# Expert weights split once beside attention, 27 units of 256 rows, and rows added into the output by accumulating scatters

## The reference, cut to what matters

```python
x = layernorm(h).reshape(-1, 512)                       # 2560 rows
top_vals, top_idx = top_k(x @ gate_w.T + gate_b, 2)
routing = softmax(top_vals)
for e in range(8):
    t = x @ w1[e].T + b1[e]                             # 1024 wide
    y = t[:, 0::2] * sigmoid(1.702 * t[:, 0::2]) * (t[:, 1::2] + 1.0)
    ye = y @ w2[e].T + b2[e]
    out += ye * sum(routing * (top_idx == e))           # zero where the row did not choose e
h = h + out
```

## Time and profile before

| | us |
|---|---|
| median of 3 runs (1957.12 to 1961.39) | 1958.84 |
| the profiled execution's own time | 1960.39 |
| its span, first to last instruction | 1958.2 |
| `build_rows`, `project` | about 420 |
| attention | 640 |
| router | 280 |
| experts | 553 |
| combine | 64 |

### The profile page before, as it was taken

How to read it: one execution, slowest core, us unless ns; L and a number is a source line. 1 busy time by engine, 2 the same in 40 slices (tenths; PEclk the granted TensorE clock), 3 DMA queues, 4 the chain that set the end, 5 groups by cost and what they waited for, 6 DMA issues and landing times. The chain is left out here.

```text
span 1958.2 us, 29274 instructions
## 1 busy us (share of the span) xinstructions
PE 1469.5 (75%) x9597; PEld 737.7 (38%) x9597; DVE 1431.0 (73%) x2171; ACT 849.2 (43%) x1520; POOL 528.8 (27%) x264
## 2 busy tenths in 40 slices
PE   0364238729999999999995146974999999999960
PEld 0343113303444444444441012452555555555530
DVE  7976989959888888888881977645666666666645
ACT  4473103313777777777775000012444444444410
POOL 4000116650000000000000122101566666665526
PEclk9876568868999999999998555555999999999985
DMA  4002005652222222222224210105665555565528
GB/s 136 1 1 78 0 0 176 231 171 75 91 89 84 93 85 90 91 86 89 87 92 138 75 31 27 54 27 172 204 203 194 193 192 188 195 197 191 180 77 276
DMA packets 143798, 228.19 MB, mean 117 GB/s; under 512 B 14478, under 2 KB 69646, under 8 KB 143706
## 3 DMA queue, kind: packets, MB, share of 16 engines
q1 hardware_dynamic: 134034, 199.31, 30.5%
q0 software_dynamic: 8752, 28.06, 5.1%
q10 hardware_dynamic: 960, 0.17, 0.0%
HBM read 163.14 MB, written 64.03 MB: 116 GB/s over the span
## 5 line engine op out<-in xcount | busy, mean ns | idle before, releaser
L1254 ACT ACTIVATE pT<-p 128x512 f32<-128x512 f32 x800 | 422.9, 609 | 153.9 <-PE p L1155 151.8
L1227 DVE TENSOR_REDUCE mxa<-p 128x1 f32<-128x512 f32 x640 | 409.8, 682 | 96.1 <-PE p L1137 96.1
L1720 POOL TENSOR_TENSOR wl<-shared,wh 128x2048 bf16<-128x2048 f32 x60 | 255.7, 4290 | 128.5 <-ACT wh L1796 128.5
L1137 PE MATMUL p<-ks,qs 128*128 128x512 bf16 x640 | 250.1, 393 | 39.8 <-DMA vs<-d_v 36.4
L1155 PE MATMUL p<-qs,ks 128*128 128x512 bf16 x640 | 243.3, 380 | 14.2 <-ACT pT L1254 12.9
L1753 PE MATMUL p<-xh,wh 128*128 128x384 bf16 x672 | 220.0, 327 | 1.2 <-DVE xl L1833 1.2
L1753 PE MATMUL p<-xl,wh 128*128 128x384 bf16 x672 | 219.9, 327 | 0.0
L1753 PE MATMUL p<-xh,wl 128*128 128x384 bf16 x672 | 219.9, 327 | 0.0
L682 POOL TENSOR_TENSOR xT<-xT,qcbb_ctx 128x2560 f32<-128x2560 f32 x4 | 17.9, 4475 | 705.9 <-DVE qcbb_ctx L700 705.9
L1173 PE MATMUL p<-pT,vs 128*32 128x128 f32 (+1 forms) x2560 | 205.5, 439 | 1.0 <-ACT pT L1254 1.0
L1850 DVE TENSOR_TENSOR yl<-yf,yh 128x384 bf16<-128x384 f32 x84 | 140.8, 1677 | 48.5 <-ACT yh L1811 48.5
(11 more groups left out here) (326 smaller groups left out, 2349.3 us busy)
## 6 DMA issues: line engine op xcount, KB each, us to landing
shared<-in_w1T SPq DMA_DIRECT2D x42, 1024.0 KB
shared<-in_w2T SPq DMA_DIRECT2D x21, 1024.0 KB
d_y<-yo SPq DMA_DIRECT2D x63, 256.0 KB, 4.8
d_v<-xT SPq DMA_DIRECT2D x20, 512.0 KB, 3.9
vs<-d_v SPq DMA_DIRECT2D x32, 320.0 KB
d_o<-osb SPq DMA_DIRECT2D x32, 320.0 KB, 2.2
d_q<-xn SPq DMA_DIRECT2D x16, 480.0 KB, 2.8
d_k<-xn SPq DMA_DIRECT2D x16, 480.0 KB, 2.8
```

The lines of the kernel that those rows point to most:

```text
L1137: mm = pe.matmul(out, qs[u][:, h, q], ks[u][:, h, 0:512], start=True, stop=True)
L1227: dve.tensor_reduce(mxa[u][:, h, qt:qt + 1], bank, AX.X, ALU.max, negate=True).then_inc(s_mfree, 1)
L1254: act.activation(dst, ps[:, second_bank(c, s)], ACT.Exp).then_inc(s_p, 1)
L1720: pool.tensor_tensor(wl[n % 2][:, k], wf[:, k], wh[n % 2][:, k], ALU.subtract).then_inc(s_wl, 1)
```

## The change

Four things are changed together.

1. **Weights.** While attention runs, GpSimd loads each of the 24 parts of 1 MB of the expert weights (8 experts, 3 parts) by a DMA of its own queue, takes hi by a cast and lo by a subtraction, and stores both to `d_w` (another 1 MB). Part n starts once `s_pv` has reached 5n + 1, one part a group. The staging tiles are `xT4`, which attention leaves free. The expert stage then loads hi and lo ready made, 3 MB of bf16 per unit, in a ring of three buffers, two units ahead, by two DMAs with long rows; ScalarE's L1796 and GpSimd's L1720 are gone.
2. **Units** have 256 slots, and there are 27. The router writes the normed rows to `d_x2` as bf16 hi and lo (ScalarE casts, GpSimd subtracts), so a gather brings both, the turns are bf16 (16 a unit), and hi and lo need no splitting behind them: one copy by ScalarE and one by VectorE, 1024 elements each, take them out of PSUM.
3. **Output.** The router stores the residual `hs` to `d_acc`, and puts into each slot its row (`slot_row`) and its probability (`slot_prob`, carried through the token product as three bf16 parts, so that product has five tables instead of two). In the expert stage VectorE multiplies the second layer by the probability and adds the weighted bias, and GpSimd adds the 128 rows to `d_acc` by an indirect DMA that accumulates in memory. Each such scatter waits for the one before it. At the end `d_acc` is copied to `out`, by two DMAs of SP and two of ScalarE; `combine` is gone.
4. `build_rows` allocates its semaphores directly and clears them behind a barrier of its own.

```diff
+        d_w = dram("d_w", (EXP_N, P, 3 * WPART), BF16)
+        d_acc = dram("d_acc", (TOK + P, L))
...
+        w_first = shared[:].bitcast(BF16)
+        s_w = [[ctx.enter_context(nc.semaphore(f"expert_weights{k}_in{c}")) for k in (1, 2)] for c in range(RING)]
...
+        def load_expert(sp, n, w, free=lambda k: None):
+
+            e = sp.value_load(unit_e[0:1, n:n + 1], min_val=0, max_val=EXP_N - 1)
+            for k, at, end in ((0, 0, 2 * WPART), (1, 2 * WPART, 3 * WPART)):
                 free(k)
-                sp.dma_start(wf[:, k], src.rearrange("e (i p) o -> p (e i) o", p=P)).then_inc(s_w, 16)
+                sp.dma_start(w[:, at:end], d_w[bass.ds(e, 1), :, at:end].rearrange("e p w -> p (e w)")
+                             ).then_inc(s_w[n % RING][k], 16)
...
-        combine(nc, a, locals())
...
+            def load(n):
+                e, k = divmod(n, 3)
+                src = a["w1T"][e, k] if k < 2 else a["w2T"][e]
+                pool.dma_start(wf[n % 2].rearrange("p (i o) -> p i o", i=IT), src.rearrange("(i p) o -> p i o", p=P)
+                               ).then_inc(s_wf[n % 2], 16)
+
+            load(0)
+            load(1)
+            for n in range(3 * EXP_N):
+                u, (e, k) = n % 2, divmod(n, 3)
+                hi, lo = wsplit[u][:, 0:IT * L], wsplit[u][:, IT * L:]
+                pool.wait_ge(s_pv, SPLIT_PACE * n + 1)
+                pool.wait_ge(s_wf[u], 16 * (n // 2 + 1))
+                if n >= 2:
+                    pool.wait_ge(s_wst[u], 16 * (n // 2))
+                pool.tensor_copy(hi, wf[u]).then_inc(s_wsp, 1)
+                pool.wait_ge(s_wsp, 2 * n + 1)
+                pool.tensor_tensor(lo, wf[u], hi, ALU.subtract).then_inc(s_wsp, 1)
+                pool.wait_ge(s_wsp, 2 * n + 2)
+                pool.dma_start(d_w[e, :, k * WPART:(k + 1) * WPART], wsplit[u]).then_inc(s_wst[u], 16)
+                if n + 2 < 3 * EXP_N:
+                    load(n + 2)
...
-UNIT = 384
+UNIT = 256
+RING = 3
+WPART = 2 * IT * L
 UNITS = (TOK * TOPK - EXP_N) // UNIT + EXP_N
...
-                sp.wait_ge(s_xn, COMPS * (b + 1))
-                sp.dma_start(d_x2[b * T:(b + 1) * T].rearrange("(c p) l -> p c l", p=P), xn[:, b % 2]).then_inc(s_x2[b % 2], 16)
+                sp.wait_ge(s_xl, COMPS * (b + 1))
+                sp.dma_start(d_x2[b * T:(b + 1) * T].rearrange("(c p) l -> p c l", p=P),
+                             xb[:, b % 2].rearrange("p c s l -> p c (s l)")).then_inc(s_x2[b % 2], 16)
+            sp.dma_start(d_acc[0:TOK].rearrange("(t p) l -> p t l", p=P), hs[:]).then_inc(s_acc, 16)
             sp.wait_ge(s_unit, 1)
-            load_expert(sp, 0)
+            load_expert(sp, 0, w_first)
...
+                if b >= 2:
+                    act.wait_ge(s_x2[b % 2], 16 * (b // 2))
+                for r in range(b * COMPS, (b + 1) * COMPS):
+                    act.wait_ge(s_xn, r + 1)
+                    act.copy(xb[:, b % 2, r % COMPS, 0], xn[:, r % COMPS]).then_inc(s_xh, 1)
...
-                mm = pe.matmul(ps[:, 2, 0:2 * COLS], lane_is[:, n], col_is[:, n].rearrange("p s c -> p (s c)"),
+                mm = pe.matmul(ps[:, 2, 0:NS * COLS], lane_is[:, n], col_is[:, n].rearrange("p s c -> p (s c)"),
...
-                    if b >= 2:
-                        dve.wait_ge(s_x2[b % 2], 16 * (b // 2))
-                        dve.wait_ge(s_turn, COMPS * (b - 1))
                     for r in range(b * COMPS, (b + 1) * COMPS):
-                        dve.tensor_scalar(xn[:, b % 2, r % COMPS], hs[:, r], mv[:, r, 0:1], sd[:, r:r + 1],
+                        if b >= 1:
+                            dve.wait_ge(s_xl, r - COMPS + 1)
+                            dve.wait_ge(s_turn, r - COMPS + 1)
+                        dve.tensor_scalar(xn[:, r % COMPS], hs[:, r], mv[:, r, 0:1], sd[:, r:r + 1],
                                           ALU.subtract, ALU.mult).then_inc(s_xn, 1)
...
+            chain(dve.tensor_copy(pparts[:, 0], prob[:]))
+            chain(dve.tensor_tensor(prest, prob[:], pparts[:, 0], ALU.subtract))
+            chain(dve.tensor_copy(pparts[:, 1], prest))
+            chain(dve.tensor_tensor(pparts[:, 2], prest, pparts[:, 1], ALU.subtract))
...
+            for n in range(3):
+                chain(dve.tensor_tensor(col_is[:, :, 2 + n], col_is[:, :, 1],
+                                        pparts[:, n].unsqueeze(2).broadcast_to([P, PAIRS, COLS]), ALU.mult))
...
+            chain(dve.tensor_scalar(idf, found[:, 1], -float(P), None, ALU.add))
+            chain(dve.scalar_tensor_tensor(idf, found[:, 0], float(P), idf, ALU.mult, ALU.add))
+            chain(dve.tensor_scalar(slot_token[:], idf, 0.0, None, ALU.max))
+            chain(dve.tensor_scalar(no_row[:], my_lane[:], float(TOK + P), None, ALU.add))
+            chain(dve.tensor_scalar(empty, found[:, 0], 0.0, None, ALU.is_equal))
+            chain(dve.scalar_tensor_tensor(slot_row[:], empty, no_row[:], idf, ALU.mult, ALU.add))
+            chain(dve.tensor_copy(slot_prob[:], found[:, 2]))
+            chain(dve.tensor_tensor(slot_prob[:], slot_prob[:], found[:, 3], ALU.add))
+            chain(dve.tensor_tensor(slot_prob[:], slot_prob[:], found[:, 4], ALU.add))
...
+            def load_weights(n):
+                def free(k):
+                    if n >= RING and k == 0:
+                        sp.wait_ge(s_g1, IT * (n - RING + 1))
+                    if n >= RING and k == 1:
+                        sp.wait_ge(s_g2, Q * (n - RING + 1))
+
+                load_expert(sp, n, w_flat[n % RING], free=free)
...
+                    sp.wait_ge(s_yo, Q * (n - RING + 1))
...
+            sp.wait_ge(s_sc, 16 * Q * NU)
+            for h in range(0, 4, 2):
+                rows = slice(h * TOK // 4, (h + 1) * TOK // 4)
+                sp.dma_start(rows_out[rows], d_acc[rows]).then_inc(s_out, 16)
+            sp.wait_ge(s_out, 16 * 4)
...
-                    pool.wait_ge(s_tx, IT * n)
+                c = n % RING
+                if n >= RING:
+                    pool.wait_ge(s_tx, Q * (n - RING + 1))
                 for q in range(Q):
...
+                    pool.indirect_dma_start(xg[c][:, q], None, d_x2, bass.IndirectOffsetOnAxis(slot_token[:, Q * n + q:Q * n + q + 1], 0)
+                                            ).then_inc(s_xg[c], 16)
 
             gather(0)
+            gather(1)
+            pool.wait_ge(s_acc, 16)
             for n in range(NU):
-                if n + 1 < NU:
-                    gather(n + 1)
-                    for k in range(3):
-                        weight_lo(n + 1, k)
+                if n + 2 < NU:
+                    gather(n + 2)
+                for q in range(Q):
+                    j = Q * n + q
+                    pool.wait_ge(s_yo, j + 1)
+                    if j >= 1:
+                        pool.wait_ge(s_sc, 16 * j)
+                    pool.indirect_dma_start(d_acc, bass.IndirectOffsetOnAxis(slot_row[:, j:j + 1], 0), yo[j % OUTS][:], None,
+                                            compute_op=ALU.add).then_inc(s_sc, 16)
...
+            def turn(i, c):
+                pe.wait_ge(s_xg[c % RING], 16 * Q * (i + c // RING + 1))
                 for q in range(Q):
...
+                n = num(i, c)
+                pe.wait_ge(s_xa, n + 1)
+                pe.wait_ge(s_xd, n + 1)
+                pe.wait_ge(s_w[c][0], 16 * (i + 1))
                 for o in range(IT):
-                    wait(pe, s_yf, i, c, IT, o - 1)
+                    if not first:
+                        pe.wait_ge(s_yf, IT * (n - 1) + o + 1)
...
+                        out = ps[:, 2 + o, k * UNIT:(k + 1) * UNIT]
...
+                                mm = pe.matmul(out, w[c][:, k, ws, t, cols], x[c][:, t, xs], start=t == 0 and m == 0,
                                                stop=t == IT - 1 and m == 2)
                     mm.then_inc(s_g1, 1)
-                pe.wait_ge(s_wl, count(i, c, 3, 3))
+                if not last:
+                    turn(i, c + 1)
+                pe.wait_ge(s_w[c][1], 16 * (i + 1))
...
+                            pe.wait_ge(s_yl, IT * n + t + 1)
+                        for m, (ws, ys) in enumerate(PRODUCTS):
+                            mm = pe.matmul(ps[:, 6 + q], y[c][:, t, ys, q * P:(q + 1) * P], w[c][:, 2, ws, t],
...
+                for q in range(Q):
+                    if not first:
+                        pe.wait_ge(s_yo, Q * (n - 1) + q + 1)
                     second(q, range(IT - 1))
-                for q in range(2):
+                for q in range(Q):
                     second(q, range(IT - 1, IT))
-                if not last:
-                    turn(i, c + 1, 2)
-                    turn(i, c + 1, 3)
-                for q in range(2, Q):
-                    wait(pe, s_yo, i, c, Q, q - 1)
-                    second(q, range(IT))
-
-            for t in range(IT):
-                turn(0, 0, t)
-            run(pe, unit)
+
+            turn(0, 0)
+            for c in range(RING):
```

(37 more changed lines are left out.)

331 lines of the change are left out of this document (109 added, 222 removed).

## The result

The changed kernel takes 1915.33 us in the median (1912.37 to 1922.42), against 1958.76 of the kernel before: the ratio is 0.9781, 95% interval 0.9762 to 0.9799, a gain of 43 us. Forecast were 1879 us in a range of 1845 to 1940 and a chance of 86% for faster. Sign and range held; the gain is 55% of the 79.5 us that the sum gave.

What follows compares the result with a forecast made beforehand. TensorE was taken to bound attention and experts, transfers the tail. Experts -82, tail -28, attention +17, router +16.5, start +1, lead-in -4 sum to -79.5 on 1960.4, 1880.9; median forecast 1879 us, range 1845 to 1940.

Steps and rivals of the forecast that it cites:

- Experts, -82: Expert stage: 27 units of 256 slots at 16.7 us, 454 us in all against 535.8 before; -82 us.
- Scatter chain: Expert stage: two scatters a unit, each issued after the last one's landing; expected hidden, 3.7 us to spare.
- S: Expert stage: time from one scatter's issue to the next, taken as 6.5 us; the chain decides from 8.3.
- Rival A: Expert stage: the chain of scatters binds and the kernel gets slower; 1922 us at 9 us a scatter, 2034 at 11; 12%.
- The bound of 8.7 us: Upper bound for a scatter's time, from the experts' third gather: issued at 1344.27, used at 1352.95.
- Rival B: Expert stage: the DMA engines bind, units take 17.6 to 19 us; +24 to +62, total 1903 to 1941; 12%.
- Tail, -28: Last expert matmul to the end: 64.7 us become 36, with last scatters 13 and copy 20; -28 (-36 to -15).
- Router and lead-in, +12.5: Router +16.5 us (added tables, wider token product, small steps, casts), less 4 before the first expert matmul.
- Attention, +17: Attention: weight splitting costs 0.6 us of TensorE a group, 15 in all, plus 2 for first loads; 0 to +43.
- the block's end (+1): Start of the kernel: one more block's end, behind build_rows, costs +1 us.
- Rival C: Attention: splitting costs more, by unabsorbed waits or its DMAs delaying the small transfer behind nm; 1905 to 1934 us; 11%.
- all of D: Attention: wording in the costlier-splitting rival, where it stood at 1.7 to 2.9 us unabsorbed.

Runs made afterwards that it cites:

- e10_third: Changed kernel with each unit's first scatter sent twice, so three chained scatters a unit (output not the reference's); 2039.00 us, ratio 1.0408.
- e1_compute: Changed kernel with all 24 casts and subtractions of the splitting but only 3 of 24 loads and stores (output not the reference's); 1868.82 us, ratio 0.9536.
- e9_spread_phase3: Changed kernel with queries and keys in twelve transfers of 16 rows instead of six, and splitting parts started two add_values later; 1853.08 us, ratio 0.9462.
- e3_phase3: Changed kernel with each splitting part started two add_values (about 7 us) later in its group; 1932.25 us, ratio 0.9832.
- e6_before_spread: Kernel before the change, with each group's queries and keys in twelve transfers of 16 rows instead of six; 1950.70 us, ratio 0.9945.

## Why the prediction was right, and where not

- **Experts, -82:** right, -87.2. The line through 384 and 512 columns gave 16.54 us a unit; measured 16.55. TensorE has no wait there. The 0.15 us a unit that I added for joints aren't there.
- **Scatter chain:** S at 6.5, "hidden, 3.7 us to spare", was wrong in its reserve. Undisturbed S is 5.6 us, under the 6.5, but beside the weights' bursts (DMA engines at 83%) it is 10.7 us in the unit shown, and 8.7 to 12 in one scatter of nearly every unit; the two fill 16.4 of 16.55 us. That the two distances add up to a unit does not measure the reserve, for a chain that keeps pace always does so. A measure is `e10_third`: a third scatter adds some 5.5 us of chain and 4.6 us to the unit, so about 1 us was to spare, an estimate, not 3.7. Rival A had 12%. The bound of 8.7 us came from idle engines and was none. Rival B is out: TensorE never waits for weights, and the DMA engines stand at 0 GB/s for 2 to 3 us in each unit (from 1613 to 1616, say).
- **Tail, -28:** right in kind, -35.4. Two scatters 10.1 us instead of 13, the copy, issued from 1895.56 on, 13.1 and 14.2 us to landing instead of 20, near the lower bound of 13.8.
- **Router and lead-in, +12.5:** +14.7. The three tables took 7.29 us against 7.1; the token product 7.48 instead of 9.4 us, at a mean granted clock of 0.64 (1411 to 1420 us) and not at the half clock of the forecast; from the last router step to the first expert matmul it is 14.9 us, 2.3 less than before instead of 4.
- **Attention, +17:** the step that failed; it is +64, the block's end (+1) included. "They bring 48 MB beside 640 us, 75 GB/s on top of 88 at 28% busy: room enough" read a mean over 16 engines, of which the group's loads use two or three. Their transfer took nearly a group's 18.5 us before the change; the splitting's traffic on the same engines made it longer, and TensorE waits for it in nearly every group. The 0.6 us a group for `nm` was right in its mechanism and too large: `nm` is held to the end of the subtraction, by 0.4 us and not 1.7, since the cast takes 1.89 us and not 3. `e1_compute`, which keeps that, is back at 583 us with 0.1 us a group. Rival C gave 1905 to 1934 and holds the result, by "the splits' DMAs" rather than by what it put first; the late transfer was the big one of the group, and the small one behind `nm` came only once the big ones were spread. (In C, "all of D" should read all of the wait of `nm`.)
- **The range:** that it held is in part luck. It was wide enough for rival C, and what experts and tail gave beyond the forecast, 12 us, hid a quarter of the 46 us that attention cost beyond it.

The spread transfers give back 49.5 us in the total (8 of them are theirs in the kernel before, too), and with the moment of issue 62.

A version that beats both kernels came of it: `e9_spread_phase3`, 1853.08 us, 5.4% under the kernel before. Its span from the first to the last `nm` is 582.3 us, 6 above the kernel before, all of it between the first two `nm` (22.65 against 16.44 us).

## What to carry to other kernels

A low mean of the DMA engines is no room: look at slices of 1 us, and where they read a tenth for many us on end, suspect a transfer on a few engines; count those, not the mean, before other traffic is put beside it, and try the transfer in blocks of 16 rows, as here. Traffic that is moved beside a tight stage also needs a place in its period, behind the small transfers on which the stage turns: here, with the spread transfers, 7 us of shift were worth 13 us, and 15 us of shift cost 50. A chain of transfers that wait for each other has its price under load, so double a link to see what is left. And a wait costs more than its own length where the granted clock falls with it: in `e3_phase3` first to last `nm` grew by 71 us, with 50 us of new waits for `vs`.

## What the runs showed of the hardware

A group's loads have the same bytes in 6 or 12 transfers, and busy share 0.28 and 0.51: the share counts the time that packets are under way, and spread packets are each under way longer, by an estimated 120 ns against 74 (0.51 and 0.28 of 16 engines for 18 us, over 1222 and 1088 packets). A high share is therefore no proof of full engines either: `e9_spread_phase3` ran attention at 0.79 without a wait of TensorE for a transfer.

```profile
710.00:728.00 18.00, 17.79 (x161) 7.68 (x160) 15.33 (x27) 13.24 (x26) 0.00 (x0) 1.00 0.28 93
```

```profile
702.00:720.00 18.00, 17.79 (x161) 7.79 (x157) 15.33 (x27) 13.39 (x26) 0.00 (x0) 1.00 0.51 92
```

```profile
700.00:900.00 200.00, 196.11 (x1726) 84.99 (x1726) 169.36 (x289) 147.33 (x279) 78.00 (x43) 1.00 0.79 197
```

These are stretches of the kernel before, of `e6_before_spread` and of `e9_spread_phase3`.
